# Expert rows turned by VectorE in 32x32 blocks, with rows and first-layer weights loaded one feature group per transfer

## The chip, the cores and the metric

One core of a Trainium2 chip runs the kernel alone. The metric is the device time of one execution in microseconds. The kernel before takes 1007.0 us in the median of three executions (1005.17 to 1007.7).

## What is computed

The reference is a decoder of two layers, with post-normalisation, on x of 8 x 100 x 512 in fp32, with a context of 8 x 722 x 512:

```python
# in order: self-attention, cross-attention, experts; latent attention, cross-attention, fp8 product
x = _layernorm(x + _L0_ffn_ref(x, ...), axis=-1)          # the third of six such lines

vals, idx = jax.lax.top_k(probs, K)                       # K = 2 of E = 8 experts, from softmax of x @ gate_w + gate_b
h = jax.nn.relu(jnp.einsum('bsd,edo->ebso', x, w1) + b1[:, None, None, :])
h = jax.nn.relu(jnp.einsum('ebso,eop->ebsp', h, w2) + b2[:, None, None, :])
y = jax.nn.relu(jnp.einsum('ebso,eop->ebsp', h, w3) + b3[:, None, None, :])
v = jnp.einsum('ebso,bse->eo', y, w_tok)                  # weighed by the gate and summed over an expert's rows
out = jnp.einsum('bse,eo->bso', ind, v)                   # a row gets the sums of its two experts
```

The change lies in the first of these layers: the rows have to stand with their features on the partitions before they can be multiplied by w1 (512x512 for each expert, fp32).

## The kernel before

The kernel is a sequence of blocks, each with its own program for every engine and a barrier at its end. Engines are ordered by semaphores alone.

A row is 512 features and 8 gate values, 520 fp32 numbers (XW = 520, 2080 bytes). Ahead of the expert stage, GpSimd scatters each row twice into DRAM (rows_dram), at the place of each of its experts. An expert's region is cut into tiles of 128 rows, and the stage works on MT = 20 tiles. Each has a first row and an expert number in a table on the chip; SP reads them into registers (value_load in expert_of and gather), and so its transfers follow the data.

The stage is the last block printed below (from line 2044). Its work is cut into units (line 1676): unit (i, l) is layer l of tile i. The order is a diagonal one: (t, 0), (t-1, 1), (t-2, 2) for t = 0, 1, ..., so there are 60 units, and from tile 2 on unit (i, 0) has the number 3i - 3.

- SP loads the weights of a unit, 1024 KB, into one of SLOTS = 6 places of w (load_unit, line 1684): partition p gets the four rows c*128 + p of the matrix, 2 KB each. Loads 0 to 2 and the first AHEAD = 6 gathers are issued in the block before (lines 1998 to 2003). In the stage, load n from 6 on waits until unit n - 6 is made. From n = 5 on a gather follows each load, one tile each, until all 20 are there; from then on one of six loads for the next layer follows each weight load (last: rk, rv, rd, ru, rw, rq, of 1024, 1024, 256, 256, 256 and 1024 KB). gather (line 1780) is one transfer of 128 rows of 2080 bytes, a row to a partition.
- TensorE turns the tile: four transposes of 128x128 through the identity into PSUM bank 3 or 4 (turn, line 2069). It does so one unit ahead of the tile's first layer. A unit is 16 products of 128x128x128 in fp32, two records each (layer, line 2102), into one of RING = 3 banks. Before each unit with l = 1 one product spreads the gate column over the partitions.
- ScalarE copies the turned tile to xh (keep, line 2142), takes the first layer out of PSUM with bias and relu (line 2150), and sums the weighed outcome (line 2158).
- VectorE takes the second layer out (line 2198), sums the gate column, and weighs the third layer by the gate (line 2213). GpSimd picks the gates of the tile (line 2247).
- Some preparation for the next layer is put in between: at unit 39 (PREP_AT) VectorE waits for rk and rv and adds them, at unit 40 ScalarE waits for rd, ru, rw and rq (line 2170).

Semaphores that the change touches: gathered (a tile's rows have landed), turned and kept (transposes made, xh written), w_landed (a load in a slot has landed).

## Time and profile before

| | before |
|---|---|
| three executions | 1007.7, 1007.0, 1005.17 us |
| profiled execution, its span | 1003.7 us |
| mean clock granted to TensorE | 0.957 |
| TensorE busy | 934.0 us (93%) |
| VectorE, ScalarE, GpSimd busy | 429.3, 346.5, 250.9 us |
| bytes moved by DMA | 162.01 MB |

The span runs from the first to the last instruction of one profiled execution. Durations come from this execution, and the times above from others. The expert stage lies between 437 and 674 us of the span. In the views an operation is named by its line, and L2113 is the matmul of layer, L2074 that of turn, L2084 the spread of the gate, L2147 the copy to xh, L2203 and L2219 VectorE's evictions, L1687 the issue of a weight load, L1782 that of a gather. Matmul records overlap: their pitch is what counts in line, not their duration. A load is a queue's work from its issue to its landing, and the DMA share is the mean share of time in which the sixteen queues had a packet open.

### The profile page before, as it was taken

What the parts mean: (1) busy time and instruction counts of PE and PEld (TensorE: products, weight loads), DVE (VectorE), ACT (ScalarE), POOL (GpSimd) and SP (SyncE); (2) the same over time, 40 slices, a digit from 0 to 9 for tenths busy, and PEclk for the clock granted to TensorE, in tenths of its full rate; (3) what the DMA queues carried; (4) which work ended last, traced back from release to release, by engine and by line L of the source; (5) the groups of instructions that cost most, each with busy time, mean ns of one, the idle gap of its engine ahead of it and who ended that gap; (6) DMA issues with size and microseconds to landing.
All of it is one profiled execution on the core that took longest, in us unless ns stands there. A gap on an engine that the chain in (4) does not pass through costs nothing. (4 is left out here: it accounts for less than half of the span.)

```text
span 1003.7 us, 19227 instructions
## 1 busy us (share of the span) xinstructions
PE 934.0 (93%) x7747; PEld 757.2 (75%) x7747; DVE 429.3 (43%) x994; ACT 346.5 (35%) x886; POOL 250.9 (25%) x306
## 2 busy tenths in 40 slices
PE   5999999989998889999999999999889899999994
PEld 5977776676775644789999999987765578999532
DVE  2973454224442647002112132135267630656576
ACT  2322323245552124122222233324276611122374
POOL 5452111023554306000000010004065403000275
PEclk9999999999999979899999999997969998999996
DMA  9994000245622807259999888700040032971001
GB/s 254 382 331 127 2 2 2 98 152 203 238 120 95 309 7 254 55 181 386 358 383 313 284 269 283 254 29 28 4 153 3 2 119 78 321 247 66 1 15 51
DMA packets 72456, 162.01 MB, mean 161 GB/s; under 512 B 4132, under 2 KB 5685, under 8 KB 70321
## 3 DMA queue, kind: packets, MB, share of 16 engines
q1 hardware_dynamic: 70048, 156.54, 45.8%
q0 software_dynamic: 2320, 4.25, 1.4%
q8 instruction: 61, 1.00, 0.4%
q14 instruction: 27, 0.21, 0.1%
HBM read 128.81 MB, written 31.97 MB: 160 GB/s over the span
## 5 line engine op out<-in xcount | busy, mean ns | idle before, releaser
L2113 PE MATMUL ps<-ffn_h,ffn_w 128*128 128x128 f32 x1280 | 149.1, 275 | 0.0
L2113 PEld LDWEIGHTS ps<-ffn_h,ffn_w 128*128 128x128 f32 x1280 | 145.9, 192 | 0.0
L2113 PE MATMUL ps<-ffn_xh,ffn_w 128*128 128x128 f32 x640 | 74.9, 275 | 0.3 <-ACT ffn_xh L2147 0.3
L2203 DVE TENSOR_SCALAR ffn_h<-ps,tile_bias 128x128 f32<-128x128 f32 x80 | 22.5, 345 | 122.4 <-PE ps L2113 122.4
L2113 PEld LDWEIGHTS ps<-ffn_xh,ffn_w 128*128 128x128 f32 x640 | 73.1, 192 | 0.9 <-issue 0.9
L1418 POOL TENSOR_TENSOR ctx_low<-shelf,ctx_high 128x1024 fp32r<-128x1024 f32 (+2 forms) x24 | 43.0, 1819 | 65.4 <-PE ps L1283 33.7
L2161 ACT ACTIVATE ffn_y<-ffn_y 128x128 f32<-128x128 f32 x80 | 23.7, 298 | 73.9 <-DVE ffn_y L2219 73.9
L1526 PE MATMUL ps<-x_qT,ctx_ct 128*128 128x100 f32 (+1 forms) x384 | 46.4, 284 | 2.3 <-PEq L137 2.0
L1526 PEld LDWEIGHTS ps<-x_qT,ctx_ct 128*128 128x128 f32 (+1 forms) x384 | 45.0, 197 | 3.7 <-issue 3.2
L2219 DVE SCALAR_TENSOR_TENSOR ffn_y<-ps,tile_bias,ffn_gate_row 128x128 f32<-128x128 f32 x80 | 22.6, 344 | 58.0 <-PE ps L2113 57.9
L2834 POOL TENSOR_TENSOR att_e<-att_e,decay 100x400 f32<-100x400 f32 x32 | 32.7, 1033 | 46.1 <-DVE att_e L2685 46.1
L111 PE MATMUL ps<-ctx_ct,x_qT 128*100 128x210 f32 (+1 forms) x128 | 40.3, 467 | 1.0 <-DVE ctx_ct L1432 0.7
L2155 ACT ACTIVATE ffn_h<-ps,tile_bias 128x128 f32<-128x128 f32 x80 | 22.8, 368 | 41.6 <-PE ps L2113 41.6
L3007 POOL TENSOR_TENSOR rstd<-rstd,minus_half 100x1 f32<-100x1 f32 x16 | 11.6, 740 | 99.6 <-DVE rstd L2950 95.0
L111 PEld LDWEIGHTS ps<-ctx_ct,x_qT 128*100 128x100 f32 x128 | 20.6, 166 | 18.7 <-issue 17.4
L2781 ACT ACTIVATE att_e<-att_e,att_mx 100x100 f32<-100x100 f32 x96 | 28.1, 365 | 15.5 <-DVE att_mx L2690 15.5
L1538 PE MATMUL ps<-ctx_pT,shelf 128*128 128x100 f32 (+1 forms) x288 | 33.2, 275 | 0.2 <-ACT xf L1571 0.2
L1538 PEld LDWEIGHTS ps<-ctx_pT,shelf 128*128 128x128 f32 (+1 forms) x288 | 32.6, 192 | 0.4 <-issue 0.4
L1565 ACT ACTIVATE ctx_pk<-ctx_pk,ctx_st 128x100 f32<-128x100 f32 x48 | 13.8, 365 | 54.9 <-DVE ctx_st L1601 54.9
L2906 PE MATMUL ps<-x_n,xf 128*100 128x512 f32 x64 | 29.9, 596 | 0.6 <-PEq L1507 0.6
L111 PE MATMUL ps<-l_ro,xf 128*100 128x512 f32 x64 | 29.7, 608 | 0.0
L2147 ACT ACTIVATE ffn_xh<-ps 128x512 f32<-128x512 f32 x20 | 11.8, 598 | 49.1 <-PE ps L2074 49.1
(469 smaller groups left out, 2096.8 us busy)
## 6 DMA issues: line engine op xcount, KB each, us to landing
ffn_w<-in_L_ffn_w_dram SPq DMA_DIRECT2D x60, 1024.0 KB, 6.0
shelf<-in_ctx_dram SPq DMA_DIRECT2D x12, 1280.0 KB
expert_rows<-nothing SPq DMA_DIRECT2D x1, 14820.0 KB, 49.6
context_turned<-ctx_ct SPq DMA_DIRECT2D x8, 1444.0 KB, 7.9
ctx_ct<-context_turned SPq DMA_DIRECT2D x8, 1444.0 KB, 12.5
ctx_lent<-in_ctx_dram SPq DMA_DIRECT2D x4, 1280.0 KB
rows_own<-expert_rows SPq DMA_DIRECT2D x8, 260.0 KB, 3.0
x_wo<-in_L_xattn_Wo_dram SPq DMA_DIRECT2D x1, 2048.0 KB, 9.5
```

Of the source, the lines that this page charges most:

```text
L111: last = pe.matmul(out, a, b, start=(n == 0), stop=(n == len(products) - 1))
L1418: nc.gpsimd.tensor_tensor(raw_low[b % RAWS][0:rows_, j0:j1, :], raw[b % RAWS][0:rows_, j0:j1, :], raw_high[b % 2][0:rows_, j0:j1, :].bitca ...
L1526: mm = nc.tensor.matmul(ps[0:rows_, SB + i, (j - j0) * T:(j - j0 + 1) * T], ct[b % 2][:, k, j * P:j * P + rows_], qT[:, k, b * T:(b + 1) * T],
L1538: mm = nc.tensor.matmul(ps[:, VB, c * T:(c + 1) * T], raw[b % RAWS][0:keys(j), j, c * P:(c + 1) * P], pT[0:keys(j), b % 2, j, :], start=j ...
L2113: mm = nc.tensor.matmul(acc(n)[:, m, :], w[:, n % SLOTS, k, m * P:(m + 1) * P], into[l][:, i % 2, k, :], start=k == 0, stop=k == C - 1, sk ...
L2155: nc.scalar.activation(h1[:, i % 2, m, :], acc(n)[:, m, :], ACT.Relu, bias=bsel[:, m, i, 0:1]).then_inc(h1_kept, 1)
L2161: nc.scalar.activation(y[:, i % 2, m, :], y[:, i % 2, m, :], ACT.Relu, accum_out=vT[:, m, i:i + 1]).then_inc(counted, 1)
L2203: nc.vector.tensor_scalar(h2[:, i % 2, m, :], acc(n)[:, m, :], bsel[:, m, i, 1:2], 0.0, ALU.add, ALU.max).then_inc(h2_kept, 1)
L2219: nc.vector.scalar_tensor_tensor(y[:, i % 2, m, :], acc(n)[:, m, :], bsel[:, m, i, 2:3], gate_row[:, i % 2, :], ALU.add, ALU.mult).then_in ...
L2781: ins = nc.scalar.activation(e[:, c, :], e[:, c, :], ACT.Exp, bias=mx[:, b % 2, r, c:c + 1])
L2834: nc.gpsimd.tensor_tensor(e, e, decay[:, :].unsqueeze(1).to_broadcast([T, C, T]), ALU.mult).then_inc(faded, 1)
L2906: mm = nc.tensor.matmul(ps[0:T, b % 3, :], xf[:, k, b * T:(b + 1) * T], n1[:, k, :], start=k == 0, stop=False)
```

## The change

- The rows of a tile are loaded in four transfers, one for each group f of 128 features, into the 32 partitions of group f. Partition 32f + r gets the pieces i*32 + r of that group, four pieces of 128 features (512 bytes) for i = 0 to 3. A fifth transfer brings the eight gate values of each row (32 bytes) to the row's own partition, on a semaphore of its own.
- VectorE transposes the whole 128x512 tile in one instruction, in blocks of 32x32, into xh. Feature f*128 + k*32 + d then lies on partition 32f + d in piece k, and the 128 rows lie in four runs of 32. The four transposes on TensorE and the copy on ScalarE are gone.
- The weights of the first layer are loaded to fit: four transfers of 256 KB, one for each f, into the 32 partitions of the group, in pieces of 2 KB as before. A slot's semaphore therefore counts four transfers for a first-layer load, and one for others (landed_by).
- The matmuls of the first layer read xh with four runs of 32 numbers for each partition.
- Three tiles are gathered ahead of the stage in place of six (EARLY), and in the stage a gather follows only the loads with odd n. The gathers thus run from n = 5 to n = 37, where before they ran from 5 to 18, and the six loads for the next layer follow loads 38 to 43, where before they followed 19 to 24.

```diff
@@ -1672,10 +1672,14 @@
         w = sb("ffn_w", [P, SLOTS, C, D], F32, ff)
-        expert_w = [g[f"L0_ffn_w{i}"].rearrange("e (c p) o -> p e c o", p=P) for i in (1, 2, 3)]
+        first_w = g["L0_ffn_w1"].rearrange("e (f k d) o -> f d e k o", f=HPC, k=C)
+        group = lambda f: slice(f * HD, (f + 1) * HD)
+        expert_w = [g[f"L0_ffn_w{i}"].rearrange("e (c p) o -> p e c o", p=P) for i in (2, 3)]
         units = [(t - l, l) for t in range(MT + NL - 1) for l in range(NL) if 0 <= t - l < MT]
...
         w_landed = [sem(f"ffn_landed{s}") for s in range(SLOTS)]
+        parts_of = lambda n: HPC if units[n][1] == 0 else 1
+        landed_by = [16 * sum(parts_of(m) for m in range(n % SLOTS, n + 1, SLOTS)) for n in range(len(units))]
@@ -1684,8 +1688,13 @@
             i, l = units[n]
-            sp.dma_start(w[:, n % SLOTS, :, :], expert_w[l][:, bass.ds(expert, 1)].rearrange("p a c o -> p (a c) o")
-                         ).then_inc(w_landed[n % SLOTS], 16)
+            if l == 0:
+                for f in range(HPC):
+                    sp.dma_start(w[group(f), n % SLOTS, :, :], first_w[f, :, bass.ds(expert, 1)].rearrange("d a k o -> d (a k) o")
+                                 ).then_inc(w_landed[n % SLOTS], 16)
+            else:
+                sp.dma_start(w[:, n % SLOTS, :, :], expert_w[l - 1][:, bass.ds(expert, 1)].rearrange("p a c o -> p (a c) o")
+                             ).then_inc(w_landed[n % SLOTS], 16)
@@ -1762,7 +1771,7 @@
                 + [("m1", m) for m in range(1, C)])
-        AHEAD = 6
+        AHEAD, EARLY = 6, 3
         wq1_hi = ([sb_at(f"x1_wq_hi{k}", [P, D], xf_at + 4 * D * k, FR) for k in range(AHEAD)]
@@ -1775,11 +1784,16 @@
         fold_bank = lambda n: ps[:, (7, 0, 1)[n % 3], :]
-        gathered = [sem(f"rows_gathered{i}") for i in range(MT)]
+        gathered, gathered_gates = ([sem(f"{what}_gathered{i}") for i in range(MT)] for what in ("rows", "gates"))
...
             row = sp.value_load(table[0:1, 1, i:i + 1], min_val=0, max_val=SPARE)
-            sp.dma_start(rows_of_tile(i), rows_dram[bass.ds(row, P), :]).then_inc(gathered[i], 16)
+            here = rows_dram[bass.ds(row, P), :]
+            for f in range(HPC):
+                sp.dma_start(rows_of_tile(i)[group(f), 0:D].rearrange("r (i d) -> r i d", d=P),
+                             here[:, f * P:(f + 1) * P].rearrange("(i r) d -> r i d", r=HD)).then_inc(gathered[i], 16)
+            sp.dma_start(rows_of_tile(i)[:, D:XW], here[:, D:XW]).then_inc(gathered_gates[i], 16)
@@ -1999,7 +2013,7 @@
                 sp.wait_ge(folded, fold_at["bvo", 0] + 1)
-                for i in range(AHEAD):
+                for i in range(EARLY):
                     gather(sp, i)
@@ -2014,14 +2028,15 @@
         RING = 3
-        xh, h1, h2 = (sb("ffn_" + n, [P, 2, C, P], F32, ff) for n in ("xh", "h1", "h2"))
+        xh = sb("ffn_xh", [P, 2, HPC, C, HD], F32, ff)
+        h1, h2 = (sb("ffn_" + n, [P, 2, C, P], F32, ff) for n in ("h1", "h2"))
         into = (xh, h1, h2)
...
         vT = sb("ffn_vT", [P, C, MT], F32, ff)
-        turned, kept, made, h1_kept, h2_kept, gated, gate_col, gate_rows, rows_kept, weighed, counted, v_flip, v_hi, v_lo, by_tile, tile_kept = (
-            sem("ffn_" + s) for s in ("turned", "kept", "made", "h1_kept", "h2_kept", "gated", "gate_col", "gate_rows",
+        kept, made, h1_kept, h2_kept, gated, gate_col, gate_rows, rows_kept, weighed, counted, v_flip, v_hi, v_lo, by_tile, tile_kept = (
+            sem("ffn_" + s) for s in ("kept", "made", "h1_kept", "h2_kept", "gated", "gate_col", "gate_rows",
                                       "rows_kept", "weighed", "counted", "v_flip", "v_hi", "v_lo", "by_tile", "tile_kept"))
@@ -2049,32 +2064,24 @@
                         (rq, natural(g["L1_attn_Wq"]), in_qup)]
-                more = AHEAD
+                more = EARLY
                 for n in range(NL, len(units)):
...
                     if n >= SLOTS - 1 and more < MT:
-                        gather(sp, more)
-                        more += 1
+                        if n % 2:
+                            gather(sp, more)
+                            more += 1
                     elif more == MT and last:
...
                 for s in range(SLOTS):
-                    sp.wait_ge(w_landed[s], 16 * (len(units) // SLOTS))
+                    sp.wait_ge(w_landed[s], landed_by[len(units) - SLOTS + s])
...
             def _(pe):
-                def turn(i):
-                    pe.wait_ge(gathered[i], 16)
-                    if i >= 2:
-                        pe.wait_ge(kept, i - 1)
-                    for c in range(C):
-                        mm = nc.tensor.transpose(ps[:, 3 + i % 2, c * P:(c + 1) * P], rows_of_tile(i)[:, c * P:(c + 1) * P],
-                                                 ident[:, :])
-                    mm.then_inc(turned, 1)
-
                 def spread_gate(i):
@@ -2101,7 +2108,7 @@
                     i, l = units[n]
-                    pe.wait_ge(w_landed[n % SLOTS], 16 * (n // SLOTS + 1))
+                    pe.wait_ge(w_landed[n % SLOTS], landed_by[n])
                     if n >= RING:
@@ -2110,15 +2117,13 @@
                                 pe.wait_ge((h1_kept, h2_kept)[l - 1], C * i + k + 1)
+                            rhs = xh[:, i % 2, :, k, :] if l == 0 else into[l][:, i % 2, k, :]
                             mm = nc.tensor.matmul(acc(n)[:, m, :], w[:, n % SLOTS, k, m * P:(m + 1) * P],
-                                                  into[l][:, i % 2, k, :], start=k == 0, stop=k == C - 1,
+                                                  rhs, start=k == 0, stop=k == C - 1,
                                                   skip_group_check=True)
...
-                turn(0)
                 for n, (i, l) in enumerate(units):
-                    if n + 1 < len(units) and units[n + 1][1] == 0:
-                        turn(units[n + 1][0])
                     if l == 1:
@@ -2140,13 +2145,6 @@
             def _(act):
-                def keep(i):
-                    act.wait_ge(turned, i + 1)
-                    if i >= 2:
-                        unit_made(act, i - 2, 0)
-                    nc.scalar.activation(xh[:, i % 2, :, :], ps[:, 3 + i % 2, :].rearrange("p (c t) -> p c t", c=C),
-                                         ACT.Identity).then_inc(kept, 1)
-
                 def first_layer(n, i):
@@ -2161,10 +2159,7 @@
-                keep(0)
                 for n, (i, l) in enumerate(units):
-                    if n + 1 < len(units) and units[n + 1][1] == 0:
-                        keep(units[n + 1][0])
                     if 0 <= n - PREP_AT - 1 < len(PREP):
@@ -2195,6 +2190,13 @@
             def _(dve):
+                def turn(i):
...
+                    dve.wait_ge(gathered[i], 16 * HPC)
+                    if i >= 2:
+                        unit_made(dve, i - 2, 0)
+                    nc.vector.transpose(xh[:, i % 2].rearrange("p i k r -> p (i k r)"), rows_of_tile(i)[:, 0:D]).then_inc(kept, 1)
...
                 def second_layer(n, i):
@@ -2219,7 +2221,10 @@
+                turn(0)
                 for n, (i, l) in enumerate(units):
+                    if n + 1 < len(units) and units[n + 1][1] == 0:
+                        turn(units[n + 1][0])
                     if l == 0:
@@ -2241,7 +2246,7 @@
                 for i in range(MT):
-                    pool.wait_ge(gathered[i], 16)
+                    pool.wait_ge(gathered_gates[i], 16)
                     if i >= 2:
```

## Rows read from the trace of the kernel before

**Rows 1.** The page: span, and slices of 25.1 us each (TensorE, clock, DMA, rate).

```profile
span 1003.7 us, 19227 instructions
...
## 2 busy tenths in 40 slices
PE   5999999989998889999999999999889899999994
...
PEclk9999999999999979899999999997969998999996
DMA  9994000245622807259999888700040032971001
GB/s 254 382 331 127 2 2 2 98 152 203 238 120 95 309 7 254 55 181 386 358 383 313 284 269 283 254 29 28 4 153 3 2 119 78 321 247 66 1 15 51
```

**Rows 2.** Groups of the stage, 437 to 674 us: count, busy us and mean ns.

```profile
L2113 PE MATMUL ps<-ffn_h,ffn_w 128*128 128x128 f32 x1280 | 149.1, 275 | 0.0
...
L2113 PE MATMUL ps<-ffn_xh,ffn_w 128*128 128x128 f32 x640 | 74.9, 275 | 0.3 <-ACT ffn_xh L2147 0.3
...
L2147 ACT ACTIVATE ffn_xh<-ps 128x512 f32<-128x512 f32 x20 | 11.8, 598 | 49.1 <-PE ps L2074 49.1
...
L2074 PE MATMUL ps<-ident,rows_own 128*128 128x128 f32 x32 | 4.7, 274 | 0.9 <-PEq L1784 0.9
```

**Rows 3.** TensorE in order of time: start, duration, line, [idle before, releaser].

```profile
437.90 1.07 PE L2074 MATMUL ps<-ident,rows_own 128*128 128x128 f32 x8 [0.94 <-PEq L1784]
439.31 3.81 PE L2113 MATMUL ps<-ffn_xh,ffn_w 128*128 128x128 f32 x32 [0.34 <-ACT ffn_xh L2147]
...
455.00 0.39 PE L2084 MATMUL ps<-ident,ffn_gate 128*128 128x128 f32 x2
455.23 3.74 PE L2113 MATMUL ps<-ffn_h,ffn_w 128*128 128x128 f32 x32
458.80 0.60 PE L2074 MATMUL ps<-ident,rows_own 128*128 128x128 f32 x4
459.24 3.74 PE L2113 MATMUL ps<-ffn_h,ffn_w 128*128 128x128 f32 x32
462.81 3.74 PE L2113 MATMUL ps<-ffn_xh,ffn_w 128*128 128x128 f32 x32
...
610.75 3.74 PE L2113 MATMUL ps<-ffn_xh,ffn_w 128*128 128x128 f32 x32
```

**Rows 4.** VectorE in order of time, one round; then a group of the stage.

```profile
459.00 1.13 DVE L2203 TENSOR_SCALAR ffn_h<-ps,tile_bias 128x128 f32<-128x128 f32 x4 [6.17 <-PE ps L2113]
463.10 1.13 DVE L2219 SCALAR_TENSOR_TENSOR ffn_y<-ps,tile_bias,ffn_gate_row 128x128 f32<-128x128 f32 x4 [2.97 <-PE ps L2113]
...
L2236 DVE TENSOR_TENSOR l_pw_lo<-bo_rows,l_pw_hi 128x512 fp32r<-128x512 f32 x1 | 0.7, 684 | 0.0
```

**Rows 5.** SP's queue in order of time: start and duration of DMA issues.

```profile
419.48 5.86 SPq L1782 DMA_DIRECT2D rows_own<-expert_rows  x6
...
438.57 2.69 SPq L1687 DMA_DIRECT2D ffn_w<-in_L_ffn_w_dram  x3
...
451.77 0.38 SPq L1687 DMA_DIRECT2D ffn_w<-in_L_ffn_w_dram  x1
452.91 0.35 SPq L1782 DMA_DIRECT2D xT_hi<-expert_rows  x1
...
505.41 2.11 SPq L2063 DMA_DIRECT2D l_raw_up_k<-in_L_attn_W_up_k_dram  x1
```

**Rows 6.** Stretches: start:end length, busy (count) by engine, PEclk, DMA share, GB/s.

```profile
12.00:18.00 6.00, 6.00 (x30) 5.48 (x28) 2.87 (x7) 2.85 (x7) 1.52 (x3) 1.00 1.05 240
442.00:493.00 51.00, 51.00 (x456) 50.53 (x455) 8.15 (x32) 14.52 (x59) 0.81 (x4) 1.00 1.03 371
493.00:516.00 23.00, 23.00 (x208) 23.00 (x207) 4.74 (x19) 6.37 (x28) 0.40 (x2) 1.00 1.05 385
560.00:620.00 60.00, 60.00 (x541) 60.00 (x540) 18.48 (x54) 20.03 (x76) 3.23 (x5) 1.00 0.86 279
```

**Rows 7.** DMA issues: KB each, median us from issue to landing.

```profile
ffn_w<-in_L_ffn_w_dram SPq DMA_DIRECT2D x60, 1024.0 KB, 6.0
...
rows_own<-expert_rows SPq DMA_DIRECT2D x8, 260.0 KB, 3.0
...
picks<-in_picks_dram SPq DMA_DIRECT2D x1, 64.0 KB, 1.7
```

## The prediction

> **What bounds the kernel now.** I began with the page: its span, and the slices of TensorE, its clock, the DMA share and the rate [rows 1]. The reader should see that from slice 17 to slice 26, where the expert stage lies, TensorE is full at full clock, and that in the first half of the same slices the DMA digits are 9 and the rate is above 350 GB/s. Two resources are near their ends at once. Next came the groups of the stage [rows 2]: 1920 matmul records of the layers at 275 ns (they overlap), the transposes of the rows, and one ScalarE copy a tile. Then TensorE in order of time [rows 3], which gives what each step is worth in line: a turn of a tile stands at 458.80 and the next layer at 459.24, so a turn takes 0.44 us of TensorE; a layer of one tile (a "unit") takes 462.81 - 459.24 = 3.57 us; the spread of the gate takes 0.23 us. Every tile thus costs 3 x 3.57 + 0.23 + 0.44 = 11.38 us, and TensorE never waits for weights: inside the stage its only waits are those at its start (0.94 and 0.34 us in [rows 3]). So TensorE sets the end of the stage.
>
> Last I read DMA. With a weight load and a gather per unit, and later with the loads for the next layer, the share is 1.03 and 1.05 and the rate 371 and 385 GB/s; with weights alone it is 0.86 and 279 [rows 6]. I take 385 GB/s as what the queues can do. A weight load of 1024 KB then takes 1.049 MB / 385 = 2.72 us, a gather of 260 KB 0.69 us. Now 2.72 + 0.69 = 3.41 us per unit stands against 11.38 / 3 = 3.79 us on TensorE: hidden, with a tenth to spare.
>
> **Part 1, the turn leaves TensorE: -8.6 us.** The 20 turns (one copy L2147 each in [rows 2]) go. Eighteen are in line at 0.44 us: 7.9 us. The first two and the wait for the copy span 437.90 to 439.31 [rows 3], 1.41 us; VectorE's first turn stands there instead, which I take at 0.7 us, so 0.7 us is gained. Sum 8.6 us. The ScalarE copies (0.60 us each, 20) are off the path, and their going earns nothing.
>
> **Part 2, the turn on VectorE: 0.** No row shows this operation. Lower bound: the 128x512 subtraction on VectorE, 0.68 us [rows 4]; upper bound: four such passes, 2.7 us. It stands between the second layer's eviction and the weighing. The eviction begins at 459.00 and ends at 460.13 [rows 4], 1.33 us after the unit before it ended (458.80); the next first layer may begin 3.57 us after that end, so the turn has 2.2 us. I take 0.7 us, since the operation streams the same elements once: hidden, with VectorE idle 2.97 us before each weighing. Queued behind the turn are the weighing and the gate sum, and behind these TensorE's banks; a gather that came late would stop all of them. ScalarE loses a copy that nobody then waits for. The Trainium skill ("VectorE: DVE Perf Modes", The three transpose paths) gives 311 ns for 128x128 in bf16; four times that, 1.2 us, is an estimate that also fits under 2.2 us, and no run here shows it.
>
> **Part 3, SP's queue: 0.** A weight issue takes 0.38 us, and 0.76 us pass between its end and the gather's issue (451.77 + 0.38 to 452.91), which is the register load [rows 5]. Per tile SP will issue 3 register loads for weights (2.3 us), 6 weight transfers (6 x 0.42 = 2.5 us), and 1.5 gathers of one register load and five transfers (1.5 x 2.8 = 4.2 us): 9.0 us against 10.94 us. It fits, and weights are asked for six units ahead. Issues that find the queue full wait (2.11 us at 505.41, [rows 5]); the transfers ahead are then running, so DMA loses nothing. Ahead of the stage three gathers of five transfers (3 x 2.8 = 8.4 us) replace six of one (from 419.5 to 425.3 in this execution); both end before 437.90.
>
> **Part 4, the transfers into 32 partitions.** This is the term that decides. The first layer's 1024 KB come as four transfers into 32 partitions each; so do the rows, in pieces of 512 bytes, and the gates come in pieces of 32 bytes. No row shows a transfer of this shape. One end is the full rate: 2.72 us. For the other I looked for a stretch with the DMA share full and the rate low: at 12 to 18 us the share is 1.05 and the rate 240 GB/s [rows 6]. Then the input rows, landing on 100 partitions, run among weights that land on 128. Packets there are open as much of the time and move less, so a transfer whose destination doesn't spread evenly over the partitions is slower at the receiving side. At 240 GB/s the load takes 4.37 us. If every two queues shared one way in, it would be half of 385, 5.45 us. I take 4.6 us: past 4.37, because here all sixteen queues write into a quarter of the partitions, and short of 5.45, because the four pieces lie on different partitions and queues that have drifted apart can overlap. A gather scales alike (0.69 x 4.6 / 2.72 = 1.17 us) and gets 0.2 us for its gates (bounds 0 and 0.4), 1.4 us in all.
>
> The Trainium skill has a rule on just this ("SBUF — State Buffer", Door 1: The DMA port swizzle): partitions 0 to 31 reach eight of sixteen ports, as do 0 to 63, with an asymptote of 218 GB/s. By it a first-layer load would take 4.8 us, an estimate, and the sum below would come out 4 us higher, at about 1018. The trace has only the uneven case above, which agrees in kind.
>
> **The sum.** Load 45, the first of tile 16, comes behind everything that is added: of the loads 3 to 45, 15 are first-layer ones (15 x 4.6 = 69.0 us) and 28 are not (28 x 2.72 = 76.2 us); 17 gathers (odd units 5 to 37; 17 x 1.4 = 23.8 us); and the six loads for the next layer (units 38 to 43), three of 1024 KB and three of 256 KB, 3.93 MB / 385 = 10.2 us. Together 179.2 us. SP issues the first at 438.57 [rows 5], and a transfer lands some 2 us after it has run (64 KB 1.7 us, 260 KB 3.0 us, [rows 7]): 619.8 us. TensorE now begins unit 45 at 610.75 [rows 3]; less 15 turns (6.6) and the start (0.7), it could at 603.4. So it waits 16.4 us in all, spread over the units from about 13 on. Beyond unit 45 three first-layer loads and eleven others, 3 x 4.6 + 11 x 2.72 = 43.7 us, stand against 14 units, over 50 us: no more waits, and nothing is won back. The stage ends 16.4 - 8.6 = 7.8 us later. The span goes from 1003.7 to 1011.5 us; the executions timed are 1007.0 in the median, 3.3 us over that span, which I keep: 1014.8, say 1015 us.
>
> The later load for the next layer adds a risk. ScalarE and VectorE need it from unit 40 on, and its last piece is asked for when unit 37 is done; they have about four units of cover before TensorE needs a bank. I price it at 0, and 4 us at most.
>
> **Rivals.** (a) The first half of the title holds and the DMA term doesn't: transfers into 32 partitions run at 385 GB/s. Then a tile needs 3 x 2.72 + 1.5 x 0.9 = 9.5 us of DMA against 10.94, TensorE never waits, and the time is 1007.0 - 8.6 = 998.4 us. For it: the queues are full at 385 GB/s now, so their own pace may be the limit; against it: the stretch at 240 GB/s. (b) The price lies between. Each 0.1 us on a first-layer load moves the wait by 1.9 us (15 x 0.1 + 17 x 0.025), so waits vanish at 3.75 us and gain and loss cancel at 4.2 us: 999 to 1008 us, middle 1004. (c) VectorE's turn takes 2.7 us, 0.5 us beyond its gap, and first layers wait for it: 20 x 0.5 = 10 us, 998.4 + 10 = 1008 us, provided DMA is cheap. Nothing speaks for it but the missing row. (d) The change does nothing: only if the turns weren't in TensorE's line, which [rows 3] excludes. The matmuls read their moving side in runs of 32 instead of 128; I price that at 0, and a per cent on 640 records (75 us busy, [rows 2]) would be 0.8 us.
>
> **How the numbers follow.** Forecast, DMA takes over as the bound of the stage with 4.2 us or more a load: chance 0.54, 1008 to 1023 us (5.0 us a load gives 1022.5; 5.45 would give 1031). Rival (a) 0.28, (b) 0.12, (c) 0.06. What a measurement tells from no change is 0.3%, 3 us. Faster by more, below 1004: (a) and half of (b), 0.34. Within: the rest of (b), (c) and the low edge of the forecast, 0.14. Slower: 0.52. As both signs hold much, the range runs from 998 to 1024 us; the forecast's own is 1008 to 1024.
>
> **What would show it.** Right: in the profile after, TensorE's first-layer matmuls have idle time ahead of them, released by the loads of ffn_w; the rate from 442 to about 600 us is below 330 GB/s at a full share; the stage from first matmul to last is longer than before although the turns are gone; waits end near tile 16. Rival (a): units follow each other at 3.57 us throughout, with a rate near 370 GB/s where a gather runs. Rival (c): idle time ahead of L2113 that ends with VectorE's transpose. The prediction is wrong in its size if the clock of TensorE falls in the gaps (it is 1.00 in every stretch of the stage now, [rows 6]) or if queues drift far enough apart to write to different partitions at once.

## The result, and the profile after

The kernel after takes 1058.8 us in the median of four executions (1052.95 to 1062.64), the kernel before 1006.1 us on the same chip (1005.0 to 1007.7): a ratio of 1.052, interval 1.047 to 1.056. It is slower by 5%. The forecast was slower by 0.8%, and 1058.8 lies outside the range. The place of the loss and its kind are the ones foretold; its size is not. Ratios below compare undisturbed executions only; of e6_w_halves the profiled execution was a disturbed one, 2% longer than its two shortest, so its times of the stage are read too high.

The page of after, with the slices of [rows 1] (now 26.3 us each):

```profile
span 1053.6 us, 19469 instructions
...
PE   6999999899998799997878777999988999999994
...
PEclk9999999999999798999999999998879999999996
DMA  9991000266518071499999999971030003982001
GB/s 270 380 348 44 2 2 1 97 225 226 218 63 309 21 230 28 137 263 244 229 230 222 243 281 273 266 234 54 1 120 31 3 2 113 318 269 90 1 9 54
```

In slices 17 to 25 the DMA digits are 9, as they were in the first half of the stage before, and the rate is 222 to 281 GB/s where it reached 358 to 386 before. TensorE's digits fall to 7 and 8 in slices 18 to 24.

The groups of the stage (430 to 735 us), to be held against [rows 2] and [rows 4]:

```profile
L2121 PE MATMUL ps<-ffn_h,ffn_w 128*128 128x128 f32 x1280 | 151.5, 278 | 21.7 <-DMA ffn_w<-in_L_ffn_w_dram 21.6
...
L2121 PE MATMUL ps<-ffn_xh,ffn_w 128*128 128x128 f32 x640 | 85.4, 298 | 24.4 <-DMA ffn_w<-in_L_ffn_w_dram 22.5 <-DVE ffn_xh L2198 1.8
...
L2198 DVE STREAM_TRANSPOSE ffn_xh<-rows_own 128x512 f32<-128x512 f32 x8 | 5.5, 700 | 47.9 <-PEq L1798 42.9 <-PE ps L2121 5.0
```

TensorE, which never waited for weights, now has 21.6 + 22.5 = 44.1 us of idle time that ends with a landing of ffn_w, and 1.8 us for VectorE's turn. The turn takes 700 ns. The same in the waits of the stage (count, us each), with the engine that needs the late loads for the next layer:

```profile
PE ps L2121 <- DMA ffn_w<-in_L_ffn_w_dram: 44.2, 29, 4.4
...
ACT l_pu_hi L2168 <- DMA l_raw_q<-in_L_attn_Wq_dram: 21.0, 1, 21.0
```

TensorE in order of time, in the form of [rows 3]:

```profile
436.61 5.44 PE L2121 MATMUL ps<-ffn_xh,ffn_w 128*128 128x128 f32 x32 [1.80 <-DVE ffn_xh L2198]
...
488.55 5.26 PE L2121 MATMUL ps<-ffn_xh,ffn_w 128*128 128x128 f32 x32 [3.01 <-DMA ffn_w<-in_L_ffn_w_dram]
...
628.43 5.29 PE L2121 MATMUL ps<-ffn_xh,ffn_w 128*128 128x128 f32 x32 [4.39 <-DMA ffn_w<-in_L_ffn_w_dram]
...
663.58 3.84 PE L2121 MATMUL ps<-ffn_xh,ffn_w 128*128 128x128 f32 x32 [1.14 <-DMA ffn_w<-in_L_ffn_w_dram]
```

Behind four of its longer waits (2.6 to 4.4 us) a first layer's 32 records take 5.3 to 6.7 us in place of 3.84: the clock granted has fallen to 1.2 GHz in the gap. The length of the wait alone doesn't tell: a wait of 3.01 us at 602 us has no such fall behind it, one of 2.07 us at 652 us has. Unit 45 begins at 663.58, so the way from the first matmul to it takes 227.0 us, against 171.4 before (610.75 - 439.31, [rows 3]). The stage as a whole is 55.9 us longer and the profiled span 49.9 us: the stage begins 2.7 us earlier in this execution, and the part behind it is 3.3 us shorter, at a granted clock of 0.92 against 0.91. In the runs below that leave the program ahead of the stage as it was, its start lies anywhere from 437.6 to 443.6 us, so differences of a few us are judged by the ratio of many executions, not by one span. Stretches of after, in the form of [rows 6]:

```profile
442.00:493.00 51.00, 46.15 (x390) 45.03 (x390) 10.72 (x36) 10.96 (x50) 0.81 (x4) 0.97 1.09 263
...
560.00:620.00 60.00, 47.07 (x400) 45.17 (x398) 12.92 (x45) 10.35 (x52) 0.81 (x4) 1.00 0.94 243
655.00:690.00 35.00, 31.98 (x276) 31.19 (x276) 12.47 (x35) 13.00 (x54) 0.94 (x3) 0.99 1.05 263
```

And two rows of its DMA issues, in the form of [rows 7], where a full load landed after 6.0 us:

```profile
ffn_w<-in_L_ffn_w_dram SPq DMA_DIRECT2D x40, 1024.0 KB, 16.0
ffn_w<-in_L_ffn_w_dram SPq DMA_DIRECT2D x80, 256.0 KB, 6.7
```

The share is full and 263 GB/s move where 371 did: the queues are as busy and carry 29% less. Loads that the change does not touch, the ones of 1024 KB, land after 16.0 us.

### The profile page after: what moved, and what is told of

It is laid out like the page before. It is cut to its first block and busy times, and to the rows that moved or that the text cites. A ratio compares the mean times of both kernels' runs of the same rounds, so it can differ in the third digit from the quotient of the medians.

```text
span 1053.6 us, 19469 instructions
## 1 busy us (share of the span) xinstructions
PE 939.0 (89%) x7667; PEld 756.0 (72%) x7667; DVE 442.5 (42%) x1014; ACT 335.2 (32%) x866; POOL 249.3 (24%) x306
## 5 line engine op out<-in xcount | busy, mean ns | idle before, releaser
L2121 PE MATMUL ps<-ffn_h,ffn_w 128*128 128x128 f32 x1280 | 151.5, 278 | 21.7 <-DMA ffn_w<-in_L_ffn_w_dram 21.6
L2121 PE MATMUL ps<-ffn_xh,ffn_w 128*128 128x128 f32 x640 | 85.4, 298 | 24.4 <-DMA ffn_w<-in_L_ffn_w_dram 22.5
L2121 PEld LDWEIGHTS ps<-ffn_xh,ffn_w 128*128 128x128 f32 x640 | 82.0, 211 | 28.0 <-DMA ffn_w<-in_L_ffn_w_dram 25.5
L2205 DVE TENSOR_SCALAR ffn_h<-ps,tile_bias 128x128 f32<-128x128 f32 x80 | 22.5, 345 | 147.3 <-PE ps L2121 147.3
L1526 PE MATMUL ps<-x_qT,ctx_ct 128*128 128x100 f32 (+1 forms) x384 | 43.1, 272 | 2.3 <-PEq L137 2.0
L1526 PEld LDWEIGHTS ps<-x_qT,ctx_ct 128*128 128x128 f32 (+1 forms) x384 | 41.7, 185 | 3.7 <-issue 3.2
L3012 POOL TENSOR_TENSOR rstd<-rstd,minus_half 100x1 f32<-100x1 f32 x16 | 11.7, 740 | 96.5 <-DVE rstd L2955 91.9
L1565 ACT ACTIVATE ctx_pk<-ctx_pk,ctx_st 128x100 f32<-128x100 f32 x48 | 13.8, 365 | 52.1 <-DVE ctx_st L1601 52.1
L111 PE MATMUL ps<-x_woT,x_wv 128*128 128x512 f32 x64 | 27.7, 594 | 0.0
```

The costliest lines, as they stand in the source:

```text
L111: last = pe.matmul(out, a, b, start=(n == 0), stop=(n == len(products) - 1))
L1526: mm = nc.tensor.matmul(ps[0:rows_, SB + i, (j - j0) * T:(j - j0 + 1) * T], ct[b % 2][:, k, j * P:j * P + rows_], qT[:, k, b * T:(b + 1) * T],
L2121: mm = nc.tensor.matmul(acc(n)[:, m, :], w[:, n % SLOTS, k, m * P:(m + 1) * P], rhs, start=k == 0, stop=k == C - 1, skip_group_check=True)
L2205: nc.vector.tensor_scalar(h2[:, i % 2, m, :], acc(n)[:, m, :], bsel[:, m, i, 1:2], 0.0, ALU.add, ALU.max).then_inc(h2_kept, 1)
```

## The experiments

The theory at the start: the price is in the transfers into 32 partitions, and it is larger than 4.6 us a load. The rivals: the number of transfers costs (SP, descriptors); the rows in pieces of 512 bytes cost; or one slow transfer holds up those behind it, so that a mix costs more than the sum of its parts.

The runs in one table. The times of the stage are read off the profiled execution, from the first matmul of a first layer to unit 45 and to the first matmul of the next block. "Clock" is half the length of the spells at 1.2 GHz up to unit 45, the most that they can cost. "Spread" is worked out from the trace: the time from the first to the last of the sixteen queues to finish a full-width weight load, median of the loads whose first queue finishes between 480 and 600 us. Stage, clock and spread come from one execution each.

| kernel | ratio (95%) | to unit 45 | whole stage | clock | spread |
|---|---|---|---|---|---|
| before | 1 | 171.4 | 234.4 | 0 | 1.3 |
| after | 1.052 (1.047, 1.056) | 227.0 | 290.3 | 11.9 | 9.0 |
| e1_w_groups | 1.048 (1.041, 1.054) | 214.6 | 279.8 | 10.2 | 9.9 |
| e2_w_fourths | 1.000 (0.998, 1.001) | 171.4 | 234.4 | 0 | 2.7 |
| e2b_w_mixed | 1.030 (1.026, 1.034) | 202.8 | 265.9 | 3.4 | 10.7 |
| e6_w_halves | 1.037 (1.033, 1.041) | 224.9 | 293.2 | 6.8 | 10.6 |
| e12_w_groups_lag | 1.019 (1.016, 1.022) | 188.4 | 252.6 | 3.4 | 1.8 |
| e3_w_whole | 0.995 (0.993, 0.998) | 174.1 | 235.8 | 1.7 | 5.6 |
| e5_rows_wide | 0.992 (0.989, 0.994) | 166.5 | 228.2 | 1.7 | 2.2 |
| e7_spread | 0.993 (0.990, 0.995) | 165.9 | 227.6 | 1.7 | 2.9 |
| e4_lag_bound | 1.036 (1.032, 1.039) | 206.5 | 268.4 | 10.2 | 2.6 |
| e9_mixed | 1.043 (1.039, 1.046) | 208.4 | 273.7 | 8.5 | 5.5 |
| e10_lag_mixed | 1.023 (1.021, 1.026) | 193.1 | 254.9 | 5.1 | 2.0 |
| e11_pace | 1.054 (1.052, 1.056) | 211.8 | 283.6 | 8.5 | 6.9 |
| e13_lag_three | 1.054 (1.052, 1.057) | 224.7 | 290.2 | 13.6 | 7.0 |

### Is it the number of transfers, or where they land?

Both kernels are the one before with the first-layer load cut into four transfers, and nothing else; they differ in the partitions of a piece.

```diff
+            for part in ([slice(f * HD, (f + 1) * HD) for f in range(HPC)] if l == 0 else [slice(0, P)]):   # e1
+            for part in ([slice(f, P, HPC) for f in range(HPC)] if l == 0 else [slice(0, P)]):              # e2
+                sp.dma_start(w[part, n % SLOTS, :, :], expert_w[l][part, bass.ds(expert, 1)]...)
```

> The kernel before, with only the first layer's weights changed: each 1024 KB load is cut into four transfers of 256 KB, one for each group of 32 neighbouring partitions. Rows, turns on TensorE and everything else stay. Theory A (a transfer confined to 32 neighbouring partitions is slow at the receiving side, and queues fall behind one another): with the changed kernel's 258 GB/s in its stretch without gathers, a first-layer load costs 3.15 MB / 258 - 2 x 2.72 = 6.7 us; the loads of the stage then sum to 18 x 6.7 + 39 x 2.72 + 14 x 0.69 + 10.2 = 247 us against some 216 us on TensorE, so 20 to 32 us slower than before. Theory B (the number of transfers on SP's queue is what costs): slower too, by the same amount as the kernel with every fourth partition. Theory C (the rows in pieces of 512 bytes are the cost): within 3 us of before.

> The same as e1_w_groups, except that the four transfers of a first-layer load take every fourth partition each (partition f, f + 4, ...): equal bytes, pieces, transfers and semaphores, but each transfer is spread over all of the memory's width. Theory A: within 3 us of before. Theory B: as slow as e1_w_groups. Theory C: within 3 us of before, as e1_w_groups.

e1 took 1050.2 us, e2 1005.7. First three stretches of e1, and its wait; then two of e2:

```profile
442.00:493.00 51.00, 46.83 (x402) 46.40 (x402) 8.14 (x32) 12.68 (x53) 0.81 (x4) 0.97 1.06 288
493.00:560.00 67.00, 51.60 (x409) 49.70 (x408) 9.27 (x36) 12.74 (x56) 0.81 (x4) 0.92 1.06 258
...
560.00:620.00 60.00, 52.47 (x441) 51.66 (x440) 9.28 (x36) 14.06 (x61) 0.81 (x4) 0.94 1.05 253
...
PE ps L2116 <- DMA ffn_w<-in_L_ffn_w_dram: 30.8, 21, 4.5
```

```profile
442.00:493.00 51.00, 50.49 (x447) 49.84 (x448) 8.46 (x34) 14.32 (x56) 1.54 (x8) 1.00 0.96 347
...
560.00:620.00 60.00, 60.00 (x540) 60.00 (x539) 17.36 (x50) 20.26 (x81) 3.24 (x5) 1.00 0.84 280
```

The count of transfers, of issues on SP and of descriptors is the same in both. Pieces on 32 neighbouring partitions cost 44 us; pieces on every fourth partition cost nothing. That removes the first rival, and SP with it. As the rows come as before in both, it also shows that the weights alone make most of the loss of after (52.7 us). In e1's last stretch (560 to 620 us) no gathers run. A tile's three loads are 3.146 MB, at 253 GB/s 12.4 us; if the two full-width ones are counted at 2 x 2.72 = 5.4 as before, the first-layer load is worth 7.0 us there, not 4.6.

Halves, with the first-layer load in two transfers, into partitions 0 to 63 and 64 to 127:

```diff
+            for part in ([slice(0, 64), slice(64, P)] if l == 0 else [slice(0, P)]):
```

> The kernel before, with each first-layer load cut into two transfers of 512 KB, partitions 0 to 63 and 64 to 127. If what counts is how many neighbours a transfer covers: 64 are twice 32, so most of the loss of e1_w_groups (44 us) is gone. If the two halves of the partitions each have one set of ways in, as the Trainium skill has it (SBUF - State Buffer, Door 1: The DMA port swizzle: 0 to 63 reach no more ports than 0 to 31): as slow as e1_w_groups, 1040 to 1055 us.

The ratio is 1.037 (1.033 to 1.041), some 1043 us against 1006, where e1 has 1.048 (1.041 to 1.054). Twice as many neighbours per transfer take about a quarter off the loss, and the intervals touch.

### What does such a transfer cost alone?

In the kernel before, the 1024 KB load of l_ro behind the stage is cut in the same way; few other transfers run beside it.

```diff
-            sp.dma_start(ro[:], natural(g["L1_attn_Wo"])).then_inc(in_ro[0], 16)
+            for f in range(HPC):
+                sp.dma_start(ro[f * HD:(f + 1) * HD], natural(g["L1_attn_Wo"])[f * HD:(f + 1) * HD]).then_inc(in_ro[0], 16)
```

> The disputed cost by itself, in a quiet stretch: the kernel before, with the 1024 KB of the attention's output weights (line 2257, issued at 674.5 us, landed 5.6 us later with nothing but 320 KB ahead of it) in four transfers into groups of 32 partitions. Theory A: the four run at half the way in, 4.8 us in place of 2.7, so the last lands 7.5 to 8.5 us after the first issue, and there is no time for a queue to fall far behind. If a narrow transfer costs 6.7 us even without other traffic: 9.5 us or more. Nothing waits for it, so the kernel's time stays.

In the one execution of this kernel (1005.5 us, no change) the four pieces landed at 680.53, 681.80, 683.01 and 684.16 us: 1.21 us for each 256 KB, 4.8 us for the whole, 217 GB/s. The packets of 2 KB then were open for 166 ns in the median, against 84 ns before. The stretch of e8, then a stretch of the load in one piece in the kernel before:

```profile
679.00:683.00 4.00, 2.49 (x9) 1.49 (x10) 2.80 (x7) 2.02 (x3) 2.37 (x8) 0.69 1.02 203
```

```profile
676.00:679.00 3.00, 1.38 (x10) 1.14 (x9) 2.90 (x7) 0.97 (x2) 1.74 (x5) 0.83 0.98 351
```

The share is 1.02, so the queues are no less busy: each packet takes twice as long. The rule quoted in the prediction from the Trainium skill ("SBUF — State Buffer", Door 1: The DMA port swizzle), eight of sixteen ports and 218 GB/s for partitions 0 to 31 and for 0 to 63 alike, agrees with 1.21 us a piece here, and nearly with the halves of e6. So alone the load costs 4.8 us, 0.2 more than the prediction took; the other 2 us of the 7.0 appear only among other traffic.

### What the other parts of the change are worth

e3 is the kernel after with the first-layer weights in one transfer over 128 partitions. For this the features are dealt out otherwise: partition p takes four neighbouring rows of the matrix, 4p to 4p + 3, and the transpose reads its row with a step of four numbers. A partition's four rows then lie side by side in DRAM and come as one piece of 8 KB, a second difference beside the width.

```diff
-        first_w = g["L0_ffn_w1"].rearrange("e (f k d) o -> f d e k o", f=HPC, k=C)
+        first_w = g["L0_ffn_w1"].rearrange("e (p k) o -> p e k o", p=P)
...
-                    nc.vector.transpose(xh[:, i % 2].rearrange("p i k r -> p (i k r)"), rows_of_tile(i)[:, 0:D])
+                    nc.vector.transpose(xh[:, i % 2], rows_of_tile(i)[:, 0:D].rearrange("p (i d k) -> p i k d", i=HPC, k=C))
```

> The changed kernel, with the first layer's weights back in one transfer over all 128 partitions: feature 128f + 4d + k now lies on partition 32f + d in piece k, so that a partition takes four neighbouring rows of the matrix (8 KB in one run), and VectorE reads the rows with a step of four numbers. The rows still come in four transfers into 32 partitions. Theory A: the weights made up most of the loss; each tile still has a gather into 32-partition groups at 1.2 to 2 us, hidden at 3 x 2.72 + 1.5 x 2 = 11.2 us a tile against 10.94 at worst. So from 8 us faster than before (all hidden) to 5 us slower, with no waits after the gathers end. Theory C: the loss stays at 30 us or more. VectorE's transpose may take longer than its 0.70 us because of the step; up to 2.2 us is hidden.

It took 1000.7 us, 5.4 less than before (its profiled execution, 1004.9 us, is one of the longest of ten, and its stage in the table is 1.4 us longer than before's). Its turn, its waits for weights, and a stretch with gathers:

```profile
L2197 DVE STREAM_TRANSPOSE ffn_xh<-rows_own 128x512 f32<-128x512 f32 x8 | 8.7, 1092 | 50.5 <-PEq L1797 45.9 <-PE ps L2120 4.6
...
PE ps L2120 <- DMA ffn_w<-in_L_ffn_w_dram: 5.7, 6, 1.4
...
516.00:560.00 44.00, 43.12 (x385) 42.83 (x384) 13.36 (x40) 10.35 (x52) 0.81 (x4) 1.00 1.07 298
```

The turn costs 1.09 us with its step, and is still hidden but for the start, where TensorE waits 2.2 us for it. The whole loss of 52.7 us is gone with the narrow weight loads; that it was their width and not the length of their pieces is what e1 and e2 show, both with pieces of 2 KB. The gathers are still narrow, and can be priced: per load there is half a gather, 1.049 + 0.133 = 1.182 MB; at 298 GB/s this takes 3.97 us, at the 313 GB/s of 442 to 493 us 3.78. Less 2.72 for the load, a gather costs 2.1 to 2.5 us, where 1.4 was taken. e5 tests this: e3 with each gather as four transfers over 128 partitions. It leaves out the sorting of the feature groups, so its stage works on features in a wrong order, and only its time is of use.

```diff
-                sp.dma_start(rows_of_tile(i)[group(f), 0:D].rearrange("r (i d) -> r i d", d=P),
-                             here[:, f * P:(f + 1) * P].rearrange("(i r) d -> r i d", r=HD)).then_inc(gathered[i], 16)
+                sp.dma_start(rows_of_tile(i)[:, f * P:(f + 1) * P], here[:, f * P:(f + 1) * P]).then_inc(gathered[i], 16)
```

> e3_w_whole, with the rows of a tile in four transfers of 64 KB over all 128 partitions each (partition = row, 128 features a transfer) in place of 32 partitions each. Equal bytes, 512-byte pieces and transfers, only the destination is wide. This leaves out the sorting of the feature groups, so the expert stage works on rows in a wrong order of features; only its time is of use. If the narrow destination is what a gather costs: the 5.7 us of waits for weights in e3_w_whole vanish, and the rate in the stage returns to about 350 GB/s where gathers run; 3 to 6 us faster than e3_w_whole. If the short pieces or the number of transfers cost: within 2 us of e3_w_whole.

It took 996.6 us, and no unit waited for weights: the rate from 442 to 493 us is 340 GB/s at a share of 0.99. Its pieces are of 512 bytes too, so the narrow destination of the gathers is what cost e3 its 5.7 us of waits, and 3 to 4 us of time (ratios 0.995 and 0.992).

e7 keeps the narrow gathers of e3 and spaces them: one after every third load, with the loads for the next layer in between, the groups issued in the order 0, 2, 1, 3, and two small products moved ahead of unit 0.

```diff
-                    if n >= SLOTS - 1 and more < MT:
-                        if n % 2:
+                    if n >= SLOTS - 1 and more < MT and n % 3 == 2:
...
-                    elif more == MT and last:
+                    elif n >= 9 and n % 3 == 0 and last:
```

> A version meant to beat both: e3_w_whole, with one gather every third load (tile i just six units before its use) in place of every second, the six loads for the next layer at loads 9, 12, ... 24 between the gathers, the groups of a gather in the order 0, 2, 1, 3, and the two small matmuls that turn the choice of tiles moved ahead of unit 0, where TensorE waits for VectorE's first transpose. A tile then needs 3 x 2.72 + 1.8 = 10.0 us of DMA against 10.94 on TensorE, with 1.7 us more in six rounds. No waits for weights expected: 1006 - 8.6 + 1 = 998 us, 996 to 1001.

It took 998.5 us, 0.7% less than before, and faster than both kernels of the case. Against e3 (0.995, 0.993 to 0.998) the intervals overlap; what the trace shows is that the waits for weights are gone. Its stretch and the one wait left to its layers:

```profile
442.00:493.00 51.00, 51.00 (x450) 51.00 (x449) 12.32 (x36) 12.25 (x55) 0.81 (x4) 0.98 1.05 356
...
PE ps L2119 <- DVE ffn_xh L2195: 0.7, 1, 0.7
```

So the idea of the change, with this pace, is worth 7.6 us once the weights come at full width. Its stage is 6.8 us shorter than before (227.6 against 234.4), of which the start at 1.2 GHz takes 1.7 back.

### Why a narrow load costs 7 us among others and 4.8 alone

The trace shows when each of the sixteen queues is done with a load. For one full-width load of after these times are, in us behind the first queue: 0.0, 0.02, 0.05, 0.07, 0.09, 0.12, 0.19, 0.29, 0.36, 0.58, 0.66, 0.67, 2.52, 2.65, 6.08, 8.7. Twelve queues are together and four are far behind, and the unit must wait for the last. In the sixteen loads that the table's median is taken from, one to seven queues are over 2 us behind the first, one to three over 4 us, and the last 6.8 to 11.7 us. Before, the spread is 1.3 us and never over 2.7. If that lag is a cause, bounding it should help, even at the price of a wait. e4 is after with such a bound: SP issues load n only when load n - 2 has landed.

```diff
+                    if n >= NL + 2:
+                        sp.wait_ge(w_landed[(n - 2) % SLOTS], landed_by[n - 2])
                     load_unit(sp, n, expert)
```

> The changed kernel, and SP also waits until weight load n - 2 has landed in full before it issues load n, so that no queue can fall more than two loads behind the others. Theory A1 (narrow transfers cost twice 2.4 us, and on top of it one or a few queues fall 8 to 11 us behind and meet the others' traffic in the wrong phase; it is this lag that took the load from 4.9 to 6.7 us): faster than the changed kernel although a wait is added. By my sum with 4.9 us a first-layer load, 1007 - 8.6 + 22 = 1020 us, and up to 1035 with bubbles behind the waits. Theory A2 (the slow queue is slow by itself, and the lag is only its trace): no faster than the changed kernel, 1055 us or more.

It took 1041.0 us: 18 us faster than after, for an added wait, and 6 us above the range that was expected. TensorE's wait, and SP's added one:

```profile
PE ps L2123 <- DMA ffn_w<-in_L_ffn_w_dram: 28.3, 14, 4.3
...
SPq L2073 <- DMA ffn_w<-in_L_ffn_w_dram: 89.5, 40, 6.3
```

The spread falls from 9.0 to 2.6 us. The same bound on e1, where only the weights are narrow:

> e1_w_groups (the kernel before with narrow first-layer loads, 44 us of loss), and SP also waits until load n - 2 has landed before it issues load n. Without lag a narrow load costs 4.8 us, as it did alone in e8_ro_groups. Up to unit 45 that is 15 x 4.8 + 28 x 2.72 + 14 x 0.69 + 10.2 + 2 = 170 us, against 171 us on TensorE; a few us are lost in the crowded units 5 to 24. If the lag of single queues is what e1_w_groups lost by: 1008 to 1020 us. If the narrow load's own price is more than alone, or the wait costs as much as it saves: 1030 us or more.

1024.1 us: 26 of e1's 44 us are gone, and it ends 4 us above the range that was expected. Its first two stretches and its wait:

```profile
442.00:493.00 51.00, 49.41 (x439) 48.74 (x438) 8.15 (x32) 13.55 (x56) 0.81 (x4) 1.00 1.04 286
493.00:560.00 67.00, 56.80 (x478) 55.42 (x478) 10.77 (x42) 14.33 (x62) 0.81 (x4) 0.95 1.05 300
...
PE ps L2118 <- DMA ffn_w<-in_L_ffn_w_dram: 12.9, 10, 5.0
```

In the first stretch a gather follows each load: 3 x (1.049 + 0.266) = 3.945 MB a tile, at 286 GB/s 13.8 us; less 5.44 and 3 x 0.69 for what is wide, the narrow load still costs 6.3 us, with the queues together. e1 has 288 GB/s in this stretch, 6.2 us by the same sum: here the bound changes nothing. It pays from 493 to 560 us, where it takes the rate from 258 to 300 GB/s. So lag is at most a part of the excess. A bound one load later, n - 3 in place of n - 2:

> The changed kernel with the wait one load later: SP waits for load n - 3 before it issues load n, so queues can be three loads apart. If the lag is what costs and grows to what is allowed, the time lies between 1041 us (two loads) and 1059 us (no bound), 1045 to 1053, with a spread of landings between 2.6 and 9 us. If what helped in e4_lag_bound was only the emptier queue as such, then 1041 or less, as the wait leaves fewer gaps in DMA.

1060.9 us, no gain at all, with a spread of 7.0 us: a miss. It lies outside both of its expectations: a cost that grows with the lag would have given 1045 to 1053 us, a gain from emptier queues as such 1041 or less. Nor does the spread order the other runs: e3 has 5.6 us and loses next to nothing, e9 has about as much (5.5) and loses 40 us. That the bound of n - 2 helps is measured twice; that it helps by keeping the queues together is argued, since it also leaves fewer loads in flight.

The order of the four pieces was tried as well, 0, 2, 1, 3 in place of 0, 1, 2, 3, so that neighbouring transfers don't lie in the same half of the partitions. The edit is one line each, `for f in (0, 2, 1, 3)`: in e1 (as e2b), in after for weights and rows (e9), and in e4 (e10).

> The same as e1_w_groups, with the four groups issued in the order 0, 2, 1, 3. Theory A in the form that partitions 0 to 63 and 64 to 127 have separate ways in: queues that are a few packets apart write to different halves, so a load is cheaper, and the time lies between before and e1_w_groups, by my guess a third of the loss gone. Theory A in the form that any 32 neighbours are alike slow, whatever is next to them, and theory B: the same as e1_w_groups within 3 us.

> The changed kernel, with its groups (weights and rows) issued in the order 0, 2, 1, 3. With the weights alone this took 16 of 44 us away. Theory A: some 16 to 22 us of the 52 go, 1037 to 1043 us. If the rows' groups behave otherwise than the weights': 1043 to 1050.

> Both at once: SP waits until load n - 2 has landed, and the groups are in the order 0, 2, 1, 3. If lag and order remove different parts of the cost, their gains add: 1041 - 16 = 1025 us. If both work on the same part (order helps because queues that are apart write to different halves, and the wait keeps them together): 1036 to 1041, as with the wait alone.

They took 1034.1, 1046.3 and 1028.8 us: 16, 12.5 and 12 us less than with the order 0, 1, 2, 3. e2b is the third of the loss that was guessed; e9 lies in the second of its two ranges. With both remedies (e10) after loses 30 of its 52.7 us, the sum of 18 and 12. In e2b the spread stays at 10.7 us, so there the order helps in some other way than by the lag; in e9 the spread falls too, from 9.0 to 5.5. That pieces for the two halves run side by side fits; no view shows it, and it is argued, not shown.

Last, after with the pace of e7 alone (the diff of e7 without the order of groups and the moved products):

> The changed kernel with narrow weights as they are, and only the pace of e7_spread: a gather every third load, the loads for the next layer at loads 9 to 24. If the stage is bound by the sum of its transfers, spreading them changes little: the transfers after unit 45, hidden before, now include four or five gathers, so 5 to 15 us less than the changed kernel, 1044 to 1054. If it was their crowding in units 5 to 43 that cost: 1035 or less.

1058.4 us, no change: a miss. What it wins up to unit 45 (211.8 against 227.0 us) it loses behind it (71.8 against 63.3), where gathers are now left, and its profiled execution is the shortest of five. This fits a stage whose end DMA sets by its sum; no run shows it by itself.

## Why the prediction was wrong in size

**The bound.** It was read rightly. TensorE set the end, with DMA a tenth behind it (3.41 of 3.79 us a unit). e2, e5 and e7 don't wait for weights; all other kernels that change the stage do.

**Part 1, the turn leaves TensorE: right.** The working gave -8.6 us, 7.9 of it behind the first matmul of a first layer; e7's stage, counted from there, shows -6.8 us with 1.7 us lost to the clock at its start, which the working did not have, and its time -7.6 us.

**Part 2, the turn on VectorE: right.** 0.70 us against 0.7 taken, under its gap of 2.2 us, and even 1.09 us in e3 stayed hidden. At the start TensorE waited 1.80 us for it where 0.7 was taken, a miss of 1.1 us. Rival (c), 2.7 us, falls. The estimate of 1.2 us drawn from the Trainium skill ("VectorE: DVE Perf Modes", The three transpose paths) was 0.5 us too high.

**Part 3, SP's queue: right.** e2 issues the same number of weight transfers and costs nothing.

**Part 4, the narrow transfers: this step failed, in its size.** The mechanism was right, and two terms of its sum, the first-layer load at 4.6 us and the gather at 1.4 us, were too small. The sum gave 181.2 us from the first matmul to unit 45 (619.8 - 438.6), the trace has 227.0; from unit 45 to the end of the stage both before (63.0) and after (63.3) are alike, as was said. The gather costs 2.1 to 2.5 us: 17 x 0.7 or more, 12 us. The first-layer load of 4.6 us costs 4.8 alone but 6.5 to 7.0 in this traffic (e1's 7.0; in after, from 655 to 690 us without gathers, 3.146 MB at 263 GB/s is 12.0 us, less 5.44 is 6.5). With 6.5 for the load and 2.1 to 2.5 for the gather the same sum reads 15 x 6.5 + 28 x 2.72 + 17 x 2.1 + 10.2 + 2 = 221.6 us to 228.4, against 227.0 measured. With the load at its price alone, 4.8, and the gather at 2.1 it reads 196.1 us: 15 us of the miss come from the gather's price and the load's price alone, and some 31 us from what a load costs beyond that among other transfers. The price of 4.6 us was read off a stretch (12 to 18 us) that holds many kinds of transfer at once, so it was no measurement of this one. It was also held down because "queues that have drifted apart can overlap": drift was entered as a relief. In the runs the queues did drift, the load cost more than alone and not less, and the one bound that took the drift away (n - 2) gave back 18 and 26 us; only the order 0, 2, 1, 3 gives a hint of the overlap that was hoped for. The upper end of 5.45 us assumed that nothing is worse than one shared way in, and the load cost 6.5 to 7.0.

**The rivals.** (a), full rate, falls with e1, and (b), 3.75 to 4.2 us a load, with the 4.8 us of e8. The late loads for the next layer, priced at 0: ScalarE waited 21.0 us for l_raw_q, but no wait of TensorE's in the stage ends with ScalarE, and the stretch from unit 45 on took as long as before, so the cover held.

**The clock.** That it might fall in the gaps was named as a way to be wrong. It did, at a cost of up to 11.9 us up to unit 45; as DMA set the pace there, most of it lies under the waits. No run separates it.

**What would show it.** Waits ahead of first layers released by ffn_w, a rate below 330 GB/s at a full share, waits that end near tile 16 (two small ones follow, 0.23 us at 675 and 0.53 us at 688): all seen.

What stays open: why single queues fall behind, and which (the trace doesn't name them in a landing), why a bound of n - 2 helps and n - 3 doesn't, and how the order of pieces helps.

## What to carry over

Before a transfer is cut, look at which partitions each piece writes: here 32 neighbours halved the rate, 64 cost nearly as much, every fourth partition cost nothing, and often (as in e3) the order of features can be chosen so that the load needs no cut at all. Price a new form of transfer in the traffic that it will run in, not alone, and let the range reach past that price: here the load cost 4.8 us alone and up to 7.0 in the mix. Where a second resource is a tenth behind the first, that tenth is the budget of a change, and it is the first term to work out.

## What the hardware showed that was not expected

- When narrow loads ran among wide ones, the last of the sixteen queues finished a full-width load 6.8 to 11.7 us behind the first (1.3 us in the median before).
- A wait added to the issuing engine made one kernel 18 us faster (e4 against after) and another 26 us (e12 against e1); one load later it gave nothing (e13).
- The order of four like transfers, 0, 2, 1, 3 for 0, 1, 2, 3, was worth 12 to 16 us.
- The 32x32 transpose of 128x512 on VectorE takes 0.70 us, and 1.09 us where its input has a step of four numbers.
